# Vision tower with mixture of experts: expert results scattered to token places inside the loop

## The reference

```python
h = relu(einsum('btc,ech->bteh', x, W1) + b1)     # C = 192, H = 768
y = einsum('bteh,ehc->btec', h, W2) + b2
out = einsum('bte,btec->btc', gates, y)           # two gates are not zero
```

## Time and profile before

| | |
|---|---|
| Median of 3 runs | 555.1 us (554.88 to 561.28) |
| The profiled execution's own time | 549.72 us |
| Its span, first to last instruction | 547.6 us |
| Mean granted TensorE clock | 0.870 of full |
| Busy: PE, DVE, ACT, POOL | 450.6, 251.1, 192.6, 92.6 us |
| Chain that ended last, by engine | PE 55%, DVE 5%, ACT 5%, POOL 3% |

### The profile page before, as it was taken

The page is one execution under the profiler, slowest core; times in us unless marked ns, Lnnn a source line. Parts: engine busy times, 40 slices in busy tenths (PEclk is TensorE's granted clock), DMA queues, the critical chain, the costliest instruction groups (busy, mean ns, idle before and its releaser), DMA issues.

```text
span 547.6 us, 10888 instructions
## 1 busy us (share of the span) xinstructions
PE 450.6 (82%) x3748; PEld 366.1 (67%) x3749; DVE 251.1 (46%) x768; ACT 192.6 (35%) x383; POOL 92.6 (17%) x115
## 2 busy tenths in 40 slices
PE   3989999976069999999999129964699999467896
PEld 3939995775069999999999115643656766366564
DVE  6436564474413434343434444276837222777202
ACT  0053203530124444444435001289324022882320
POOL 1000127314630000000000475700001000001000
PEclk9987968775569999999999658997969999859899
DMA  8995005100312121212121221200000000000001
GB/s 290 369 418 216 1 7 167 35 1 33 115 40 62 39 64 37 66 35 67 34 67 34 69 65 44 75 16 2 2 1 0 24 24 0 4 1 1 1 0 46
DMA packets 29749, 35.16 MB, mean 64 GB/s; under 512 B 9340, under 2 KB 25719, under 8 KB 29335
## 3 DMA queue, kind: packets, MB, share of 16 engines
q1 hardware_dynamic: 26070, 28.74, 15.9%
q0 software_dynamic: 3072, 5.61, 3.7%
q10 hardware_dynamic: 576, 0.39, 0.2%
HBM read 27.01 MB, written 8.40 MB: 65 GB/s over the span
## 4 chain that ended last, share of the span: by engine, by line
PE 55%; DVE 5%; ACT 5%; issue 3%; POOL 3%; DMA 1%; SPq 0%; POOLq 0%; DVEq 0%; ACTq 0%
PE ps L767 11%; PE ps L749 9%; PE ps L794 7%; PE ps L755 5%; PE ps L924 4%; PE ps L884 4%; PE ps L806 2%; DVE sc L1451 2%; PE ps L863 2%; ACT sc L1051 2%; PE ps L618 2%; PE ps L820 2%; PE ps L925 2%; PE ps L875 1%; ACT sc L1044 1%
## 5 line engine op out<-in xcount | busy, mean ns | idle before, releaser
L767 PE MATMUL ps<-w,hidT 128*128 x384 | 65.1, 326 | 0.0
L767 PEld LDWEIGHTS ps<-w,hidT 128*128 128x128 f32 x384 | 62.0, 190 | 0.0
L749 PE MATMUL ps<-xsT,low_now 128*128 128x128 f32 x384 | 51.1, 284 | 0.9 <-ACT xsT L979 0.9
L749 PEld LDWEIGHTS ps<-xsT,low_now 128*128 128x128 f32 x384 | 47.3, 196 | 3.2 <-ACT xsT L979 1.3
L940 ACT COPY xT<-ps 96x400 f32<-96x400 f32 x32 | 15.0, 489 | 95.9 <-PE ps L618 95.9
L1003 ACT ACTIVATE hidT<-ps,b_act_now 128x128 f32<-128x128 f32 x96 | 28.2, 364 | 58.2 <-issue 53.4
L1364 DVE TENSOR_SCALAR hidT<-ps,b_dve_now 128x128 f32<-128x128 f32 x96 | 27.8, 345 | 44.4 <-PE ps L755 43.8
L618 PE MATMUL ps<-ident,x_tok 128*96 128x128 f32 x128 | 22.7, 337 | 27.7 <-DVE x_tok L1163 27.7
L644 PE MATMUL ps<-w_tok,patches 128*128 128x192 f32 x192 | 36.5, 356 | 8.8 <-DMA patches<-in_patches 8.8
L586 POOL DMA_INDIRECT y_first<-ys_dram,y_rows x16 | 16.4, 1026 | 155.4 <-DMA ys_dram<-ys 151.0
L544 POOL TENSOR_TENSOR rstd<-meanvar,eps 128x4 f32<-128x4 f32 x16 | 3.2, 198 | 232.9 <-DVE meanvar L1156 232.8
(11 more groups left out here) (206 smaller groups left out, 785.8 us busy)
## 6 DMA issues: line engine op xcount, KB each, us to landing
patches<-in_patches SPq DMA_DIRECT2D x3, 1536.0 KB, 12.0
w<-in_W SPq DMA_DIRECT2D x8, 576.0 KB, 9.7
xs<-xs_dram SPq DMA_DIRECT2D x36, 96.0 KB, 1.9
w_low<-in_W_low SPq DMA_DIRECT2D x8, 384.0 KB, 9.3
ys_dram<-ys SPq DMA_DIRECT2D x32, 96.0 KB, 1.6
patches<-in_patches SPq DMA_DIRECT2D x2, 768.0 KB, 8.1
w_high<-in_W_high SPq DMA_DIRECT2D x8, 192.0 KB, 9.6
out<-out_tok SPq DMA_DIRECT2D x8, 150.0 KB
```

What stands on the lines that cost most here:

```text
L749: pe.matmul(ps[:, 4 + 2 * v + m // 3, P * (m % 3):P * (m % 3) + P], low_now[v][:, P * m:P * m + P], xsT[v][:, 0, :], start=(m % 3 == 0), s ...
L767: mm = pe.matmul(ps[:, 2 * v + 1, 0:D], hidT[v][:, m, :], w2[:, bass.ds(experts[v], 1), D * m:D * m + D].rearrange("p e n -> p (e n)"), st ...
```

## The change

Each row of `xs_dram` grows from 192 to 194 elements: element 192 carries the token's place (tile times 128 plus partition) and element 193 the rank value of its first expert. DVE fills both into `x2_tok` in layer one. `all_rows` and the whole computation of `y_rows` go.

In the loop, DVE computes for every tile where its 128 results belong: the place, plus 2048 where the tile's expert isn't the token's first choice. It does so from `xs` in `next_place`, one iteration ahead, and copies the result as integers to `y_place_now`. This block stands between the copies of the next weights and the bias adds. SP's load of new rows into `xs` now also waits for the place (`y_place_done`). SP stores no `ys` any more; POOL scatters each `ys` tile with an indirect DMA to its places in `ys_dram`, which has 4096 rows now, first choices in one half and second ones in the other. POOL counts finished scatters up in `ys_free`, on which DVE waits before it overwrites the place and `ys` of an iteration later.

After the loop SP loads `y_first` and `y_second` in plain blocks, one DMA for each chunk and choice (512 rows, 384 KB), and POOL gathers nothing. Rows of `ys_dram` that belong to no token are filled with zeros once, early.

Also, TensorE's order for tile v = 1 in the loop is turned: first the high 64 features, then the low 128. Tile v = 0 keeps low, then high.

```diff
-        xs_dram = nc.dram_tensor("xs_dram", (ROWS, D), F32, kind="Internal").ap()
-        ys_dram = nc.dram_tensor("ys_dram", (MOE_TILES * P, D), F32, kind="Internal").ap()
+        xs_dram = nc.dram_tensor("xs_dram", (ROWS, ROW), F32, kind="Internal").ap()
+        ys_dram = nc.dram_tensor("ys_dram", (2 * Y_ROWS, D), F32, kind="Internal").ap()
...
 SP
+                sp.dma_start(ys_dram[:, :].rearrange("(s t) d -> s t d", t=HALF)[:, T:HALF, :],
+                             repeat(zeros[0:2 * Y_ROWS // HALF, 0:D], HALF - T)).then_inc(null_zero, 16)
...
                 with sp.Fori(0, MOE_TILES // 2) as tt:
                     for v in range(2):
                         sp.wait_ge(xsT_in_psum, 2 * tt + v + 3)
+                        sp.wait_ge(y_place_done, 2 * tt + v + 3)
                         row = sp.value_load(load_row_int[0:1, bass.ds(2 * tt + 4 + v, 1)], min_val=0, max_val=ROWS - P)
                         load_rows(v, row)
-                    for v in range(2):
-                        sp.wait_ge(ys_done, YS0 + 2 * tt + v + 1)
-                        sp.dma_start(ys_dram[bass.ds((2 * tt + v) * P, P), :], ys[v][:, :]).then_inc(ys_stored, 16)
-                sp.wait_ge(ys_stored, STORED0 + 16 * MOE_TILES)
+                for v in range(2):
+                    sp.wait_ge(ys_stored[v], 8 * MOE_TILES)
...
+                def load_ys(c):
+                    for k in range(2):
+                        first = k * Y_ROWS + c * TILES * P
+                        sp.dma_start((y_first, y_second)[k][c % 2][:, :, :],
+                                     ys_dram[first:first + TILES * P, :].rearrange("(i p) d -> p i d", p=P)
+                                     ).then_inc(gathered[k][c % 2], 16)
+                for c in range(2):
+                    load_ys(c)
+                for c in range(2, CHUNKS):
+                    sp.wait_ge(moe_added, c - 1)
+                    load_ys(c)
...
 POOL (fetch and its calls are gone)
+                for tt in range(MOE_TILES // 2):
+                    for v in range(2):
+                        pool.wait_ge(y_place_now_done, 2 * tt + v + 1)
+                        pool.wait_ge(ys_done, YS0 + 2 * tt + v + 1)
+                        nc.gpsimd.indirect_dma_start(
+                            out=ys_dram[:, :], out_offset=bass.IndirectOffsetOnAxis(ap=y_place_now[v][:, 0:1], axis=0),
+                            in_=ys[v][:, :], in_offset=None, bounds_check=2 * Y_ROWS - 1,
+                            oob_is_err=False).then_inc(ys_stored[v], 16)
+                    for v in range(2):
+                        pool.wait_ge(ys_stored[v], 16 * tt + 16)
+                        pool.sem_inc(ys_free, 1)
...
 PE
+                        if v == 0:
+                            low(True)
+                            mm = high(False)
+                        else:
+                            high(True)
+                            mm = low(False)
...
 DVE, layer one
+                        dve.wait_ge(place_done, 1)
+                        nc.vector.tensor_copy(x2_tok[u][:, :, D], place[:, bass.ds((2 * cc + u) * TILES, TILES)])
                         norm_apply(1, u, lambda i: tile_of(h, cc, u, i), n)
...
                         nc.vector.tensor_scalar(rows[u][:, :, :], row_sum[u][:, :, :], valid[:, 0:1], skip[:, 0:1],
-                                                ALU.mult, ALU.add)
-                        nc.vector.tensor_scalar(all_rows[:, :, bass.ds((2 * cc + u) * TILES, TILES)], row_sum[u][:, :, :],
-                                                valid[:, 0:1], skip[:, 0:1], ALU.mult, ALU.add).then_inc(rows_done, 1)
+                                                ALU.mult, ALU.add).then_inc(rows_done, 1)
...
 DVE, before and in the loop (the lines that made y_rows are gone)
+                def next_place(v, tile, n):
+                    nc.vector.tensor_scalar(is_second[v][:, :], xs[v][:, D + HALF + 1:D + HALF + 2], tile_expert[:, tile],
+                                            float(E), ALU.add, ALU.not_equal).then_inc(is_second_done, 1)
+                    dve.wait_ge(is_second_done, n)
+                    nc.vector.scalar_tensor_tensor(y_place[v][:, :], is_second[v][:, :], second_part[:, 0:1],
+                                                   xs[v][:, D + HALF:D + HALF + 1], ALU.mult,
+                                                   ALU.add).then_inc(y_place_done, 1)
...
+                    dve.wait_ge(ys_free, FREE0 + 2 * tt)
+                    dve.wait_ge(xs_in, 64 * tt + 128)
+                    for v in range(2):
+                        dve.wait_ge(y_place_done, 2 * tt + v + 1)
+                        nc.vector.tensor_copy(y_place_now[v][:, :], y_place[v][:, :]).then_inc(y_place_now_done, 1)
+                        dve.wait_ge(y_place_now_done, 2 * tt + v + 1)
+                        next_place(v, bass.ds(2 * tt + 2 + v, 1), 2 * tt + v + 3)
                     for v in range(2):
                         e = dve.value_load(tile_expert_int[0:1, bass.ds(2 * tt + v, 1)], min_val=0, max_val=E - 1)
-                        dve.wait_ge(ys_stored, 32 * tt + 16)
                         dve.wait_ge(ys_in_psum, YSP0 + 2 * tt + v + 1)
```

112 lines of the change are left out of this document (54 added, 58 removed).

## The result

The changed kernel takes 540.1 us (median of 4 runs, 537.42 to 542.28) where the kernel before, run beside it, takes 555.0 (553.68 to 561.28). The ratio is 0.9708, with a 95% interval of 0.9621 to 0.9794: faster, by 15 us on the medians. The forecast was 545.1, 10.0 less than before. Between the two profiled executions the gain is 549.72 - 537.42 = 12.3 us (spans 547.6 and 535.6), and it is this one that can be read stage by stage.

The account below looks back on a forecast made before the run. TensorE was taken to bound the expert loop, with nothing covering the hand-over to layer two. Order -3.7, hand-over -6.1 and layer one -0.2 made -10.0: 549.72 to 539.7 profiled, carried to a 545.1 us median; range 540 to 554.

Parts of the forecast that it names:

- TensorE's order: Expert loop, tile v=1: two fewer array switches save 0.23 us per iteration, at most 0.3; -3.7 us over sixteen iterations.
- Place block and SP's wait: Loop, S being an iteration's first matmul group: SP's first load S+8.9, fourth S+11.1, landed S+12.9, 0.4 us before the transposes.
- the forecast's own sign of being wrong in kind: TensorE waiting in the loop at all, or its idle stretch after the loop staying above 19 us.
- rival 1: Loop: the place comes half a microsecond too late, TensorE waits for rows, the loop gives back 4.0; 549.1 us, chance 0.16.
- Free, with 0.65 us left: DVE in the loop: the 1.7 us inserted for two place computations fit in the 3.9 us it idled.
- rival 2: Loop: place, SP's wait, four loads and transposes become the bound; slower once the excess passes 1.25 us; 557.9, chance 0.07.
- 8e: Loop cost if rows come late: the excess e is paid once in two iterations, so eight times over the loop.
- rival 4: DVE and POOL share a port: every loop scatter takes 1.59 us, hand-over 1.2 worse; 546.3 us, chance 0.07.
- Hand-over: Between loop and layer two: plain blocks instead of gathers cut TensorE's idle from 21.97 to 15.9 us, -6.1 us.
- Everything in the first pair moves along: Layer two behind the hand-over: TensorE's first-pair work only starts earlier, with no further gain or loss counted.
- the carry to the median: Whole kernel: median of runs taken as 1% above the profiled execution, turning 539.7 into 545.1 us.
- The second pair's gathers are hidden: Layer two: POOL's gathers for the second pair run beside other work, so removing them was counted at nothing.

Follow-up runs that it names:

- e1: Kernel before, only TensorE's order for tile v=1 turned to high, then low; 570.4 us, ratio 0.995, beside 571.5 for the kernel before.
- e12: Changed kernel, second tile's same products cut into six pieces, so six array switches per iteration instead of two; 554.8 us, ratio 0.971.
- e4: Changed kernel without edit, run on a chip where the kernel before takes 571.5 us; 546.6 us, ratio 0.956.
- e11: Changed kernel with six more small linked VectorE operations per iteration, behind the place block; 549.9 us, ratio 0.962.
- e10: Changed kernel with six more small linked VectorE operations per iteration, ahead of the place block; 556.8 us, ratio 0.970.
- e8: Changed kernel with 56 dummy TensorE products between loop and layer two; 544.1 us, ratio 0.950.
- e2: Changed kernel with the old order, low then high for both tiles; 549.7 us, ratio 0.963.
- e3: Kernel before without any POOL gathers, SP loading plain blocks after the loop, so results don't reach their tokens; 546.8 us, ratio 0.959.
- e9: Kernel before, unchanged, traced on a chip where it takes about 575 us; 583.0 us, one run.
- e5: Kernel before, POOL gathering only the first pair's rows, the second pair's loaded by SP in plain blocks; 555.6 us, ratio 0.971.
- e6: Kernel before, POOL gathering only the second pair's rows, the first pair's loaded by SP in plain blocks; 562.2 us, ratio 0.985.
- e7: Kernel before, POOL's second-pair gathers held back until the first squares of attention; 579.3 us, ratio 1.014.
- e13: Kernel before, second pair's gathers replaced by twenty short POOL additions, its rows loaded in plain blocks; 550.2 us, ratio 0.996.
- e16: Kernel before, keeping eight of the second pair's sixteen gathers, the rest loaded in plain blocks; 556.2 us.
- e14: Kernel before, second pair's sixteen gathers turned into plain loads issued by POOL; 555.2 us, beside 549.9 for the kernel before.
- e18: Kernel before, second pair's sixteen gathers again turned into plain POOL loads, in another group; median of two runs 554.7 us.
- e15: Kernel before with one short POOL addition ahead of each second-pair gather; 552.5 us, ratio 1.003.

## Why the prediction was right and where it was wrong

**TensorE's order: mechanism right, size too small.** The term was -3.7 us, from 0.23 a turn for two switches. e1, which does this and nothing else, shows 0.35 a turn and 5.5 us over the loop; e12 confirms the price from the other side. The sum was made from seams alone, start of the next group minus the loads' busy time, and from one low group alone: the other one in the earlier trace rows is followed by the next after 1.43 us, with a seam of 0.01, so the four seams were not alike. The rows had more to say: 24 high loads take 1.42 us in one group, now, while twelve took 0.75, so 0.08 us of start-up lie within each group's own length. The bound of 0.3 per iteration that I gave was below the truth, too.

**Place block and SP's wait: it fits, as forecast, barely.** Forecast: place ready for SP's first load at S+8.9; measured, from the first group at 176.20, 184.72 or S+8.5, and the fourth load at S+10.8 against S+11.1. TensorE waited once in sixteen iterations on the first chip, for 0.5 us, so the forecast's own sign of being wrong in kind ("if TensorE waits in the loop at all") came up, at next to no cost; pitch 8.79 on average instead of e1's 8.75, and the loop 0.7 us longer. The 3.9 us that e4 lost are not rival 1, since TensorE waits for xs there only once, for 0.2 us: the forecast had no term for late counts of TensorE. "Free, with 0.65 us left" on VectorE held: e11's pads took 0.86 from it, and it still waited for TensorE. e10 shows rival 2's chain at work. Its loop is 7.6 to 8.6 us longer than those of the changed kernel on such chips (147.0 in e8, 146.0 in e4), and TensorE waits 8.0 us in all ahead of the transposes. That is the forecast's 8e with e near 1.

**Scatters and the port.** Every one of the 32 scatters takes 0.97 to 0.98 us, so rival 4's price wasn't paid. But none of them runs beside a high_now copy, which is the meeting that rival 4 is about: the scatters of this iteration lie at 186.34 to 188.59, and the order of the loop has the copies elsewhere in all sixteen. What the Trainium skill says of the port ("SBUF — State Buffer", section "SBUF: two separate sides") was not put to the test.

**Hand-over: right.** Forecast TensorE idle 15.9 us, measured 15.48, and 15.96 and 15.30 in e4 and e2. From TensorE's end to SP's first block 4.7 us instead of 5.5; from there to the first add 3.6, where 3.1 was taken; from second add to the transposes 5.8 against 5.92. e3 gives the price of scattering instead of storing: 2.0 to 2.7 us of idle, forecast as 3.

**Behind the hand-over: a term left out.** "Everything in the first pair moves along" put the clock at nothing, and missed 1.2 us: the same products ran at a granted clock of 0.79 instead of 0.74 in the first unit. What sets it is open. The length of the idle stretch alone doesn't: after 13.3, 15.3 and 16.0 us of it (e3, e2, e4) the unit took 13.7, 14.3 and 13.7 at 0.83 to 0.87, after 15.5 here 15.1.

**What failed in the sum for this chip: the size, and the carry to the median.** The sum of -10.0 was 2.3 us short of the 12.3 between the traced executions: -4.8 for -3.7 in the loop (e1 shows that the switches' price was the part too small), -6.5 for -6.1 in the hand-over, -1.2 for nothing in the first unit, and +0.5 ahead of the loop for -0.2. The larger part of the miss is the next step. From 539.7, forecast for a traced execution, to the median the forecast added 5.4 us, the distance of the kernel before. For the changed kernel that distance is 2.7 (537.42 to 540.1). The kernel before lay wholly above its traced execution (553.68 to 561.28 against 549.72), and taking the traced one as 1% below any median was a step without a reason. The two together make the 5.0 us between 545.1 and 540.1. Why the spread differs isn't shown.

**"The second pair's gathers are hidden": the step that fails on other chips.** In the trace that I had it is true: second stretch 54.1 with and without. In three of the six groups of runs it is false: e9 and e1 show this place held for 18.8 and 17.9 us, e5 frees it by taking those gathers away and nothing else, e6 brings it back, e7 moves it. There the change is worth 25 us (e4), not 10. What the change brings in its place is not free there either: its loop scatters, of the same form, stop nobody for long, but TensorE's counts are late beside them and e4's loop loses 3.9 us. The spread of the kernel before on the first kind of chip is probably not this hold-up: e13, without these gathers, spreads from 547.2 to 563.1 as the kernel before does beside it (548.1 to 561.4).

**What stays open.** On the slower chips, semaphore counts of TensorE come late while POOL's indirect DMAs are under way, and this holds ACT and DVE; that much the traces show. TensorE itself is slowed too: in e7 it starts three to six products for the scores every 0.75 to 1.5 us while the gathers run, where 48 of them take 0.90 in e16. Whether both have one cause, which resource it is, whether plain DMAs of POOL do the same (e14 and e18 met no such chip), and why some chips show it, I can't say. All times here come from executions that the profiler recorded, so its own part isn't told apart either.

## What to carry to other kernels

A stretch of back-to-back indirect DMAs that one trace shows as hidden may be hidden on that chip only; price it once at its full length, and ask for a trace from a second chip before counting its removal at nothing. When engines that have nothing in common start at the same instant, compare the time at which the work they wait for was done with the time at which its semaphore was counted up. Price a switch between array shapes by comparing the pitch of a long group with that of two short ones, not by the visible seam. In a loop with one bounding engine, write down how much every other engine has left per turn, and look in the trace for who really ended the wait when the turn grows: e11's operations stood on VectorE, and the turn grew by a wait of ACT's.

## What the runs showed of the hardware

- The same kernel, unchanged, took 550 to 555 us in three groups of runs and 571 to 576 in three others, each group on one chip. In the one trace of it from the slower groups, one place is 18.8 us longer.
- On the slower chips, while POOL's indirect DMAs were under way, TensorE's counts of a semaphore came 9.4 to 14.1 us after the start of the product that makes them (e6, e9, e1; 0.26 in the first trace and in e15), and 0.67 to 0.68 in the loop (e8, e4; 0.30 in the first chip's trace).
- Going between products over 128 rows and over 64 rows of the array costs 0.17 to 0.20 us each time in this loop, on average (e1, e12).
- After 12.6 us of full clock and a pause of 3.4 us, the granted clock was 0.60 for the next 7.9 us (e8).
- Of four blocks of 384 KB in rows of 768 bytes, issued within 1.5 us, the first let the first add start 3.6 us after its issue, and the second add never waited for the second.
